# A two-attention, two-expert-layer kernel on one core: second-half result rows gathered by rank under the last pairs

## The chip, the cores and the metric
One core of a Trainium2 chip (trn2). The metric is the device time of one execution in microseconds, median of 3 runs; lower is better.

## What is computed
2048 tokens of 256 features go through attention a, an expert layer, attention b (with latent keys and values) and the expert layer again, each on the layer-normed input and added to it. Cut to the expert layer, on which the change works:

```
logits = x @ gate_w.T
topv, topi = jax.lax.top_k(logits, TOP_K)            # 8 of 64 experts
rw = jax.nn.softmax(topv.astype(jnp.float32), axis=-1)
W = jnp.zeros((N, E)).at[jnp.arange(N)[:, None], topi].set(rw)
gu = jnp.einsum('nh,eih->nei', x, gu_w); gate, up = (gu[..., :I], gu[..., I:])
inter_w = jax.nn.silu(gate) * up * W[:, :, None]
out = jnp.einsum('nei,ehi->nh', inter_w, dp_w)       # I = 64, H = 256
out = out + sigmoid(x @ sh_gate1_w.T) * shared_expert(x)
```

## The kernel before
The engines run five instruction streams that meet only at semaphores. In an expert layer the tokens are worked on in two halves of 8 tiles of 128: first tiles 8 to 15 (half 0), then tiles 0 to 7 (half 1). For each half, the 8192 (token, expert) slots are sorted by expert into blocks of 128 rows, each expert's share rounded up, 128 blocks at most. Two blocks are a pair: pairs 0 to 63 are half 0, pairs 64 to 127 half 1.

- GpSimd (`experts_pool`, L951 on) gathers the sorted token rows by indirect DMA, 64 of 128 rows a half, into a ring of 5 tiles (L1004). TensorE turns each (`turn`, L1368), and ScalarE stores it in `tokensT` (`store`, L1163). Half 1's tiles take the places of half 0's, so their store waits for the pair that read them.
- Per pair: the weights of two experts are copied from `weights` into `fetched` (ring of 3) by ScalarE (`fetch`, L1153) and, for the second block from pair `OTHER_FROM` = 32 on, by DVE (`other`, L1848). TensorE's `gate_up` (L1393), ScalarE's `silu` (L1170), DVE's `gate` (L1858, two operations), TensorE's `down` (L1410), ScalarE's `out` (L1176) into one of two `outs` buffers, and a store of 256 KB from SyncE to `expert_rows` in HBM (L811).
- The sum over a token's 8 experts: for tile t and rank k (the ranks are a token's rows from the last to the first, rank 0 the largest row number) GpSimd gathers 128 rows of `expert_rows` into the same ring (L1009), and DVE adds them to `x`, times the weight (`combine`, L1872). 64 such gathers and adds per half, tile by tile. A gather waits for its ring slot to be added. Half 0's begin when its stores have landed, after the token gathers; half 1's wait for the last store of all.
- Three `rstd` steps for the next norm (`inverse_std`, L947 and L949) stand between half 1's gathers, eight normalisations (L1903) after its 17th add.

The order on TensorE, ScalarE and DVE is not written by hand. `expert_plan` walks its streams of steps, always takes the step that could start first by its table `COST` and its `needs`, and returns the three orders; GpSimd's order is fixed in `experts_pool`. The DVE steps `weights` (L1798 to L1805: routing weights, 16 pieces a half) are among them. Attention b follows: SyncE loads its weights behind the last `down` (L850), and GpSimd splits them after its last `rstd` step.

## Time and profile before
| | us |
|---|---|
| median of 3 runs | 2164.07 (2158.47 to 2185.86) |
| profiled execution, its own time | 2170.09 |
| its span | 2166.8 |
| TensorE / DVE / ScalarE / GpSimd busy | 1704.3 / 1501.8 / 1108.7 / 706.8 |
| mean granted TensorE clock | 0.848 of full |

PE is TensorE, PEld its weight loads, ACT ScalarE, POOL GpSimd, SP SyncE; a q behind a name is the engine's own queue. Spans and starts are in us from the first instruction. A busy share says little of what a stage waits for; that is in the chain, the waits and the timeline of the stage. The counts of instructions are per kernel, so for both layers. "remote" and "issue" are idle times with no releaser that the trace names.

### The profile page before, as it was taken

How to read it: one execution, taken by the hardware profiler on the slowest of the kernel's cores; microseconds unless marked ns; L12 is line 12 of the kernel's file. 1: busy time of each engine (PE TensorE's matmuls, PEld its weight loads, DVE VectorE, ACT ScalarE, POOL GpSimd, SP SyncE). 2: the span in 40 equal slices, each digit the busy share in tenths (PEclk: the TensorE clock that was granted, in tenths of full speed). 3: DMA queues.
4: the chain of work that ended last, by engine and by line, in shares of the span. 5: the costliest groups of instructions: out<-in, count | busy, mean ns of one | idle time of the engine just before them, and what ended most of it. 6: DMA issues, size and time to landing. Idle time of an engine off the chain costs nothing.

```text
span 2166.8 us, 36690 instructions
## 1 busy us (share of the span) xinstructions
PE 1704.3 (79%) x12464; PEld 1097.7 (51%) x12464; DVE 1501.8 (69%) x3241; ACT 1108.7 (51%) x1975; POOL 706.8 (33%) x778
## 2 busy tenths in 40 slices
PE   5799999999767787980197999999997677788920
PEld 4545454445545666770174454544446456677720
DVE  6588888884676744984465788788844767447843
ACT  2145858566355655760041557475662456565710
POOL 5000101001266364547730001010011664554556
PEclk9778989899888999995595789798897789999965
DMA  4640223000444555664244404040004345456643
GB/s 152 139 63 2 38 25 50 12 2 2 175 151 144 161 169 160 209 197 127 68 135 86 56 2 56 6 53 8 2 2 175 121 131 165 152 165 191 207 144 114
DMA packets 123276, 217.59 MB, mean 100 GB/s; under 512 B 16380, under 2 KB 92044, under 8 KB 118812
## 3 DMA queue, kind: packets, MB, share of 16 engines
q1 hardware_dynamic: 98520, 148.10, 25.3%
q0 software_dynamic: 24576, 67.14, 11.1%
q8 instruction: 106, 1.74, 0.4%
q14 instruction: 74, 0.61, 0.1%
HBM read 124.20 MB, written 90.46 MB: 99 GB/s over the span
## 4 chain that ended last, share of the span: by engine, by line
PE 54%; DVE 15%; issue 7%; POOL 7%; DMA 7%; another core or an unknown queue 4%; ACT 4%; SPq 1%; DVEq 1%; ACTq 0%; POOLq 0%
PE late_banks L1575 13%; PE late_banks L1533 11%; PE exp_banks L1561 7%; PE late_banks L1393 6%; PE exp_banks L1410 5%; POOL ring_t L1009 5%; DVE chunk_max_t L1974 3%; DMA expert_rows<-outs_t 3%; PE late_banks L1426 3%; DVE inter_t L1858 2%; PE late_banks L1368 2%; PE late_banks L1539 2%; PE exp_banks L1426 2%; DVE hot_t L1688 2%
## 5 line engine op out<-in xcount | busy, mean ns | idle before, releaser
L1225 ACT ACTIVATE probs_t<-exp_banks 128x1024 f32<-128x1024 f32 (+3 forms) x640 | 538.8, 896 | 342.3 <-PE exp_banks L1561 340.7
L1974 DVE TENSOR_REDUCE chunk_max_t<-late_banks 128x1 f32<-128x512 f32 (+1 forms) x960 | 602.8, 683 | 106.3 <-PE late_banks L1533 86.3
L1084 POOL TENSOR_SCALAR_AFFINE_SELECT probs_t<-probs_t 128x512 f32<-128x512 f32 x128 | 81.2, 635 | 866.6 <-ACT probs_t L1225 866.6
L1393 PE MATMUL late_banks<-tokensT_t,fetched_t 128*128 x2048 | 310.1, 298 | 23.4 <-ACT fetched_t L1153 14.1
L1575 PE MATMUL late_banks<-probs_t,values_t 128*32 128x512 f32 (+3 forms) x2560 | 320.4, 576 | 9.9 <-POOL probs_t L1084 9.5
L1004 POOL DMA_INDIRECT ring_t<-token_rows,index_t x256 | 258.4, 1009 | 201.4 <-PE late_banks L1368 122.8
L1009 POOL DMA_INDIRECT ring_t<-expert_rows,rows_of_t x256 | 243.5, 951 | 196.7 <-DVE x_sb_t L1872 107.7
L1393 PEld LDWEIGHTS late_banks<-tokensT_t,fetched_t 128*128 128x128 f32 x2048 | 267.6, 204 | 52.3 <-issue 39.0
L1858 DVE TENSOR_TENSOR inter_t<-late_banks,silu_t 64x256 f32<-64x256 f32 x512 | 217.3, 424 | 109.3 <-ACT silu_t L1170 60.8
L1533 PE MATMUL late_banks<-contextT_t,Qp_t 50*128 50x512 f32 (+7 forms) x640 | 245.5, 526 | 23.2 <-DVE part_lo_t L1915 10.8
L1410 PE MATMUL exp_banks<-fetched_t,inter_t 64*128 64x128 f32 x2048 | 195.1, 312 | 69.2 <-DVE inter_t L1858 51.9
L1533 PE MATMUL late_banks<-Kp_t,Qp_t 50*128 50x512 f32 (+7 forms) x640 | 221.9, 468 | 2.3 <-DVE chunk_max_t L1974 0.9
L1176 ACT ACTIVATE outs_t<-exp_banks 128x512 f32<-128x512 f32 x256 | 152.0, 594 | 128.6 <-PE exp_banks L1410 59.0
L1410 PEld LDWEIGHTS exp_banks<-fetched_t,inter_t 64*128 64x128 f32 x2048 | 144.0, 199 | 111.4 <-DVE inter_t L1858 63.0
L1872 DVE SCALAR_TENSOR_TENSOR x_sb_t<-ring_t,row_top_t,x_sb_t 128x256 f32<-128x256 f32 x256 | 122.6, 479 | 111.9 <-DMA ring_t<-expert_rows,rows_of_t 106.2
L1533 PEld LDWEIGHTS late_banks<-contextT_t,Qp_t 50*128 50x128 f32 (+1 forms) x640 | 117.2, 226 | 142.0 <-DVE chunk_max_t L1974 94.2
L1533 PEld LDWEIGHTS late_banks<-Kp_t,Qp_t 50*128 50x128 f32 (+1 forms) x640 | 104.5, 203 | 130.9 <-DVE chunk_max_t L1974 98.9
L1153 ACT ACTIVATE fetched_t<-weights_t 128x384 f32 x320 | 158.5, 517 | 15.9 <-issue 13.5
L1561 PE MATMUL exp_banks<-Qp_t,contextT_t 52*128 52x512 f32 (+7 forms) x640 | 149.2, 438 | 16.2 <-DMA Qp_t<-neg_lo_t 12.3
L1848 DVE COPY fetched_t<-weights_t 128x384 f32 x192 | 84.7, 441 | 107.4 <-remote 55.7
L1561 PE MATMUL exp_banks<-Qp_t,Kp_t 52*128 52x512 f32 (+7 forms) x640 | 148.4, 430 | 7.2 <-ACT probs_t L1225 4.9
L1170 ACT ACTIVATE silu_t<-late_banks 64x256 f32<-64x256 f32 x256 | 95.0, 372 | 109.2 <-PE late_banks L1393 63.1
(222 smaller groups left out, 2008.1 us busy)
## 6 DMA issues: line engine op xcount, KB each, us to landing
expert_rows<-outs_t SPq DMA_DIRECT2D x256, 256.0 KB
weights_t<-in_experts SPq DMA_DIRECT2D x8, 1728.0 KB, 14.0
Qp_t<-q_parts SPq DMA_DIRECT2D x36, 256.0 KB
weights_t<-in_experts SPq DMA_DIRECT2D x4, 2112.0 KB, 9.6
Kp_t<-k_parts SPq DMA_DIRECT2D x24, 256.0 KB
q_parts<-part_hi_t SPq DMA_DIRECT2D x16, 256.0 KB, 2.6
q_parts<-part_lo_t SPq DMA_DIRECT2D x16, 256.0 KB, 3.2
k_parts<-part_hi_t SPq DMA_DIRECT2D x16, 256.0 KB, 3.0
```

The source lines that it names most:

```text
L1004: pool.indirect_dma_start(ring[:, slot, :], None, token_rows[f][:, :], bass.IndirectOffsetOnAxis(ap=index[h][:, n:n + 1], axis=0))\
L1009: pool.indirect_dma_start(ring[:, slot, :], None, expert_rows[f][h][:, :], bass.IndirectOffsetOnAxis(ap=rows_of[:, t, k:k + 1], axis=0))\
L1153: act.activation(fetched[:, n % NFETCH, blk, :], weights[:, bass.ds(fetches[n][blk], EW)], ACT.Copy)\
L1176: act.activation(outs[:, out % NOUT, :, :].rearrange("p b (s c) -> p s b c", s=2), down_banks(n).rearrange("p s (b c) -> p s b c", b=2), A ...
L1225: act.activation(probs[:, e % NP, 2 * p:2 * p + 2, off:QB], exp_banks[sq % 2][:, :, off:QB], ACT.Exp, scale=D ** -0.5).then_inc(exp_done, 1)
L1393: last = pe.matmul(bank[:, blk * P:(blk + 1) * P], fetched[:, n % NFETCH, blk, k * P:(k + 1) * P], tokensT[:, bass.ds(starts_of[n][blk] + ...
L1410: last = pe.matmul(down_bank(n, side)[:, blk * P:(blk + 1) * P], inter[rows, n % 2, blk * P:(blk + 1) * P], fetched[rows, n % NFETCH, blk, ...
L1533: last = pe.matmul(bank[:, begin:end], Qp[s][rows, p, t * P:(t + 1) * P], Kp[s][rows, p, c * QB:c * QB + end - begin], start=True, stop=c < b)
L1561: last = pe.matmul(exp_banks[sq % 2][:, hh, off:QB], Kp[s][rows, p, j * P:(j + 1) * P], Qp[s][rows, p, b * QB + off:(b + 1) * QB], start=T ...
L1575: last = pe.matmul(pv_banks[n % NPV][32 * h:32 * h + 32, off:QB], values[:, j, GH * g + h, :], probs[:, e % NP, h, off:QB], start=(j == 0) ...
L1858: dve.tensor_tensor(inter[side * EI:(side + 1) * EI, n % 2, :], up, silu[0:EI, n % 2, :], ALU.mult)\
L1974: op = dve.tensor_reduce(chunk_max[:, slot, p, r, c], bank[:, 0:n].rearrange("q (p k) -> q p k", p=len(parts)), AX.X, ALU.max)
```

## The change
1. `late_order`: half 1's 64 result gathers go by rank, not by tile: ranks 7 to 3, eight tiles each (40), then ranks 2 to 0, one block of four tiles after the other (24). They are issued behind half 0's gathers, in GpSimd's order. Each waits for pair 96 + i/2 to have read its tokens, since 63 of them land in `tokensT`, whose tiles are free by then, and the last in the ring. Two groups of two are open at most.
2. A rank of the first five waits only for the stores up to the largest row that it gathers. These marks are made on the chip: `turn_rows`, `last_rows`, `mark_row` and `marks` (two small TensorE products, six DVE operations), with GpSimd reading them into registers. Ranks 2 to 0 wait for all stores.
3. Half 1's adds leave the planner: DVE does them behind the last pair, after the eight normalisations. Half 0's 64 adds stay in the plan.
4. In half 1, ScalarE copies both weight blocks of every other two pairs (`both_copied`); DVE keeps the rest.
5. The planner's costs are others (landing 2.4 for 2.2, store 3.2 for 2.6, fetch 1.15 for 1.0, and so on), and a store of half 1's tiles is no longer planned 2.5 us behind its pair. Weight pieces 16 to 31 wait for `turn_rows`.
6. `expert_rows` of half 1 is one buffer for both layers, `last_rows_out`; attention a's ScalarE stream fills it once with finite numbers (16 DMAs of 1 MB). Attention b's weights are loaded at add 26 of half 1.

The diff, cut to its core:

```diff
@@ -63,7 +63,10 @@
-GATHERS = 4 * NG
+GATHERS = 3 * NG
+LATE_STEP, LATE_GROUP, LOADED_FROM = 3, 2, 26
+LATE_OPEN = 2
+TURN_ROWS, MARK_ROW = 33, 37
@@ -72,6 +75,7 @@
+BOTH_OF = 4
@@ -280,12 +284,25 @@
+def both_copied(n):
...
+    return n < OTHER_FROM or n >= NPAIR and n % BOTH_OF < 2
...
+def late_order():
...
+    order = [(t, k) for k in range(TOPK - 1, LATE_STEP - 1, -1) for t in HALVES[1]]
+    for b in range(HT // TPB):
+        order += [(t, k) for k in range(LATE_STEP - 1, -1, -1) for t in HALVES[1][b * TPB:(b + 1) * TPB]]
+    return order
...
-    LAND, STORED, LOADED, SIGNAL, BEHIND = 2.2, 2.6, 6.0, 0.15, 2.5
-    COST = {"gather": 1.25, "turn": 0.45, "gate_up": 1.2, "down": 0.75, "index": 0.65, "table": 0.6, "fetch": 1.0,
-            "store": 0.4, "silu": 0.4, "out": 0.61, "gate": 0.86, "other": 0.58, "columns": 3.4, "low": 1.25, "high": 1.2, "index_out": 0.3,
-            "places": 2.2, "table_out": 0.5, "rows": 2.2, "shares": 4.0, "weights": 1.4, "combine": 0.5}
+    LAND, STORED, LOADED, SIGNAL = 2.4, 3.2, 6.0, 0.15
+    COST = {"gather": 1.27, "turn": 0.45, "gate_up": 1.2, "down": 0.75, "index": 0.65, "table": 0.6, "fetch": 1.15,
+            "store": 0.4, "silu": 0.4, "out": 0.61, "gate": 0.88, "other": 0.6, "columns": 3.4, "low": 1.29, "high": 1.42, "index_out": 0.3,
+            "places": 2.2, "table_out": 0.5, "turn_rows": 0.4, "mark_row": 0.4, "last_rows": 1.0, "marks": 1.2, "rows": 2.2, "shares": 4.0, "weights": 1.4, "combine": 0.5}
@@ -303,8 +322,8 @@
                ("dve", [("gate", n) for n in pairs]),
-               ("dve", [("other", n) for n in pairs if n >= OTHER_FROM]),
-               ("dve", [("combine", n) for n in range(2 * NG)]),
+               ("dve", [("other", n) for n in pairs if not both_copied(n)]),
+               ("dve", [("combine", n) for n in range(NG)]),
@@ -363,7 +392,7 @@
             if n >= NG:
-                yield "gate_up", n // 2, BEHIND
+                yield "gate_up", n // 2, 0.0
@@ -565,7 +604,8 @@
         token_rows = [nc.dram_tensor(f"token_rows{f}", [S, E], F32).ap() for f in range(2)]
-        expert_rows = [[nc.dram_tensor(f"expert_rows{f}{h}", [NBLK * P, E], F32).ap() for h in range(2)] for f in range(2)]
+        last_rows_out = nc.dram_tensor("last_rows_out", [NBLK * P, E], F32).ap()
+        expert_rows = [[nc.dram_tensor(f"expert_rows{f}", [NBLK * P, E], F32).ap(), last_rows_out] for f in range(2)]
@@ -745,7 +791,18 @@
+        def late_tile(i):
...
+            at = i % KC * (SLOTS + P) + i // KC * E
+            return tokensT[:, at:at + E] if i < NG - 1 else ring[:, 0, :]
@@ -846,7 +907,7 @@
                 if layer == 1:
-                    sp.wait_ge(down_done, layer * PAIRS)
+                    sp.wait_ge(combined, layer * 2 * NG - NG + LOADED_FROM)
@@ -986,15 +1047,12 @@
                 slot, h, n = m % NRING, m // NG % 2, m % NG
-                place = pool_norms.get(m)
-                if place is not None:
-                    inverse_std(pool, norm_of["f", f] + 1, place)
...
-                    pool.wait_ge(rows_ready, 2 * f + h + 1)
-                    for i in range(NOUT):
-                        pool.wait_ge(outs_out[i], 16 * ((f * 2 * NPAIR + (h + 1) * NPAIR - i + NOUT - 1) // NOUT))
+                    pool.wait_ge(rows_ready, 2 * f + 2)
+                    for out in outs_out:
+                        pool.wait_ge(out, 16 * ((f * PAIRS + NPAIR) // NOUT))
@@ -1009,7 +1067,34 @@
                         .then_inc(ring_in[slot], 16)
-            for place in range(3, NB):
+            pool.wait_ge(rows_ready, 2 * f + 2)
+            pool.wait_ge(marked, f + 1)
...
+            written = [*low_marks, *high_marks]
+            for i, (t, k) in enumerate(LATE):
+                if i in LATE_NORMS:
+                    inverse_std(pool, norm_of["f", f] + 1, LATE_NORMS[i])
+                pool.wait_ge(gate_up_done, f * PAIRS + NPAIR + NPAIR // 2 + i // 2 + 1)
+                if i % LATE_GROUP == 0 and i >= LATE_OPEN * LATE_GROUP:
+                    pool.wait_ge(late_in[i // LATE_GROUP - LATE_OPEN], 16 * LATE_GROUP * (f + 1))
+                if i == NG - 1:
+                    pool.wait_ge(combined, f * 2 * NG + NG)
+                if i < (TOPK - LATE_STEP) * HT:
+                    if i % HT == 0:
+                        for out in outs_out:
+                            pool.wait_ge(out, written[k])
+                elif i == (TOPK - LATE_STEP) * HT:
+                    for out in outs_out:
+                        pool.wait_ge(out, 16 * ((f + 1) * PAIRS // NOUT))
+                pool.indirect_dma_start(late_tile(i), None, expert_rows[f][1][:, :],
+                                        bass.IndirectOffsetOnAxis(ap=rows_of[:, t, k:k + 1], axis=0))\
+                    .then_inc(late_in[i // LATE_GROUP], 16)
+            for place in range(2, NB):
@@ -1038,6 +1123,8 @@
                     inverse_std(pool, 0, b)
+                if layer == 1:
+                    pool.wait_ge(combined, layer * 2 * NG)
@@ -1149,7 +1236,7 @@
                         act.wait_ge(down_done, f * PAIRS + n - NFETCH + 1)
-                    for blk in range(2 if n < OTHER_FROM else 1):
+                    for blk in range(2 if both_copied(n) else 1):
@@ -1232,6 +1319,10 @@
                         act.activation(sums[:, n % 2, :], pv_banks[n % NPV][:, :], ACT.Copy).then_inc(sums_out, 1)
+                        if layer == 0:
+                            rows = slice(n * NBLK * P // len(BLOCKS), (n + 1) * NBLK * P // len(BLOCKS))
+                            act.dma_start(last_rows_out[rows, :].rearrange("(p r) e -> p (r e)", p=P),
+                                          values[:, 0:TPB, :, :].rearrange("p t h d -> p (t h d)")).then_inc(rows_set, 16)
@@ -1356,6 +1447,17 @@
                     table_row(1, BANK[3])
+                elif kind == "turn_rows":
+                    pe.wait_ge(out_ready, f * PAIRS + TURN_ROWS + 1)
+                    pe.wait_ge(row_done[1], HT * (f + 1))
+                    tiles = slice(HALVES[1].start, HALVES[1].stop)
+                    pe.transpose(BANK[3][0:NEXP, PW:PW + P], row_top[:, tiles, :].rearrange("p t k -> p (t k)"), ident[:, :])\
+                        .then_inc(rows_turned, 1)
+                elif kind == "mark_row":
+                    pe.wait_ge(out_ready, f * PAIRS + MARK_ROW + 1)
+                    pe.wait_ge(mark_step, 5 * f + 2)
+                    pe.matmul(BANK[3][:, PW + P:PW + P + NEXP], last_rows, ident[EI:P, EI:P], start=True, stop=True)\
+                        .then_inc(mark_product, 1)
@@ -1790,6 +1897,8 @@
                 h, first = i // PIECES, i % PIECES * EQ
+                if i == PIECES:
+                    dve.wait_ge(rows_turned, f + 1)
@@ -1812,7 +1921,28 @@
-            others = {}
+            def last_rows_of():
...
+                dve.wait_ge(rows_turned, f + 1)
+                dve.tensor_reduce(last_row, BANK[3][0:NEXP, PW:PW + P], AX.X, ALU.max).then_inc(mark_step, 1)
+                dve.wait_ge(mark_step, 5 * f + 1)
+                dve.tensor_scalar(last_rows, ident[EI:P, :], 0.0, last_row, ALU.mult, ALU.add).then_inc(mark_step, 1)
...
+            def marks_of():
...
+                dve.wait_ge(mark_product, f + 1)
+                dve.tensor_reduce(row_steps[0], BANK[3][0:1, PW + P:PW + P + NEXP].rearrange("o (t k) -> o k t", t=HT), AX.X, ALU.max)\
+                    .then_inc(mark_step, 1)
+                dve.wait_ge(mark_step, 5 * f + 3)
...
@@ -1860,11 +1996,11 @@
                 elif kind == "combine":
-                    h, t, k = n // NG, HALVES[n // NG][n % NG // TOPK], n % TOPK
+                    t, k = HALVES[0][n // TOPK], n % TOPK
...
-                    if n % NG == 0:
-                        dve.wait_ge(weights_done, 2 * f + h + 1)
+                    if n == 0:
+                        dve.wait_ge(weights_done, 2 * f + 1)
@@ -1874,10 +2010,23 @@
                         statistics(phase, t // TPB)
-                    if n == NG + 16:
-                        dve.wait_ge(down_done, (f + 1) * PAIRS)
-                        for b in MIDDLE[0:2]:
-                            normalise(phase, b)
+            dve.wait_ge(down_done, (f + 1) * PAIRS)
+            for b in MIDDLE[0:2]:
+                normalise(phase, b)
+            dve.wait_ge(weights_done, 2 * f + 2)
+            last = {}
+            for i, (t, k) in enumerate(LATE):
+                n = f * 2 * NG + NG + i
+                if i % LATE_GROUP == 0:
+                    dve.wait_ge(late_in[i // LATE_GROUP], 16 * LATE_GROUP * (f + 1))
+                if t in last:
+                    dve.wait_ge(combined, last[t])
+                dve.scalar_tensor_tensor(out=x[:, t, :], in0=late_tile(i), scalar=weight8[:, t, k:k + 1],
+                                         in1=x[:, t, :], op0=ALU.mult, op1=ALU.add).then_inc(combined, 1)
+                last[t] = n + 1
+                if k == 0 and t % TPB == TPB - 1:
+                    dve.wait_ge(combined, n + 1)
+                    statistics(phase, t // TPB)
```

How the order moves. GpSimd, layer 0, from the second token gather of half 1 on; `token_rows` are the tokens, `expert_rows` and `last_rows_out` the pairs' results. Before:

```order
L1004 DMA ring_t<-token_rows,index_t 128x256 [waits tile_turned] x63
L1009 DMA ring_t<-expert_rows,rows_of_t 128x256 [waits outs_out1,tile_turned,outs_out0,rows_ready]
L1009 DMA ring_t<-expert_rows,rows_of_t 128x256 [waits tile_turned] x4
L1009 DMA ring_t<-expert_rows,rows_of_t 128x256 [waits combined] x59
L1009 DMA ring_t<-expert_rows,rows_of_t 128x256 [waits outs_out1,combined,outs_out0,rows_ready]
L1009 DMA ring_t<-expert_rows,rows_of_t 128x256 [waits combined] x7
L947 TENSOR_SCALAR var_eps_t<-mean_var_t 128x4 [waits aggr_done]
L949 TENSOR_TENSOR rstd_t<-var_eps_t,minus_half_t 128x4 [waits eps_done]
L1009 DMA ring_t<-expert_rows,rows_of_t 128x256 [waits combined] x4
L947 TENSOR_SCALAR var_eps_t<-mean_var_t 128x4 [waits aggr_done]
L949 TENSOR_TENSOR rstd_t<-var_eps_t,minus_half_t 128x4 [waits eps_done]
```

And now:

```order
L1062 DMA ring_t<-token_rows,index_t 128x256 [waits tile_turned] x63
L1067 DMA ring_t<-expert_rows,rows_of_t 128x256 [waits outs_out1,tile_turned,outs_out0,rows_ready]
L1067 DMA ring_t<-expert_rows,rows_of_t 128x256 [waits tile_turned] x4
L1067 DMA ring_t<-expert_rows,rows_of_t 128x256 [waits combined] x59
L1072 TENSOR_LOAD silu_t [waits marked,rows_ready]
L1075 TENSOR_LOAD silu_t
L1094 DMA tokensT_t<-last_rows_out,rows_of_t 128x256 [waits outs_out1,outs_out0,gate_up_done]
L1094 DMA tokensT_t<-last_rows_out,rows_of_t 128x256 [waits gate_up_done] x3
L1008 TENSOR_SCALAR var_eps_t<-mean_var_t 128x4 [waits aggr_done]
L1010 TENSOR_TENSOR rstd_t<-var_eps_t,minus_half_t 128x4 [waits eps_done]
L1094 DMA tokensT_t<-last_rows_out,rows_of_t 128x256 [waits late_in0,gate_up_done]
L1094 DMA tokensT_t<-last_rows_out,rows_of_t 128x256 [waits gate_up_done]
```

The 64 gathers of half 0 (waiting for `combined`) stay where they were; the 64 behind them wait for `gate_up_done` instead of `combined`.

DVE around pairs 102 to 104 of layer 0, where L1872 (now L2008) is an add, L1858 (now L1994) a pair's gate and L1848 (now L1984) a weight copy. Before:

```order
L1872 SCALAR_TENSOR_TENSOR x_sb_t<-ring_t,row_top_t,x_sb_t 128x256
L1858 TENSOR_TENSOR inter_t<-late_banks,silu_t 64x256 x2
L1843 TENSOR_LOAD silu_t
L1848 ISA
L1848 COPY fetched_t<-weights_t 128x384
L1872 SCALAR_TENSOR_TENSOR x_sb_t<-ring_t,row_top_t,x_sb_t 128x256
L1858 TENSOR_TENSOR inter_t<-late_banks,silu_t 64x256 x2
```

And now:

```order
L1994 TENSOR_TENSOR inter_t<-late_banks,silu_t 64x256 x2
L1984 ISA
L1984 COPY fetched_t<-weights_t 128x384
L2008 SCALAR_TENSOR_TENSOR x_sb_t<-ring_t,row_top_t,x_sb_t 128x256 x2
L1994 TENSOR_TENSOR inter_t<-late_banks,silu_t 64x256 x2
L2008 SCALAR_TENSOR_TENSOR x_sb_t<-ring_t,row_top_t,x_sb_t 128x256 x2
L1994 TENSOR_TENSOR inter_t<-late_banks,silu_t 64x256 x2
L2008 SCALAR_TENSOR_TENSOR x_sb_t<-ring_t,row_top_t,x_sb_t 128x256 x2
L2041 BN_STATS stats_t<-x_sb_t 128x6 x4
L2044 BN_AGGR mean_var_t<-stats_t 128x2 x4
```

Before, one add a pair, and copies in each; now one or two adds at each gate, copies in two pairs of four, and half 0's adds are over here (the statistics are its last block's).

DVE behind the last pair of layer 0: L1903 (now L2052) is the normalisation. Before:

```order
L1858 TENSOR_TENSOR inter_t<-late_banks,silu_t 64x256 x2
L1872 SCALAR_TENSOR_TENSOR x_sb_t<-ring_t,row_top_t,x_sb_t 128x256 x17
L1903 TENSOR_SCALAR xn_t<-x_sb_t,mean_var_t,rstd_t 128x256 x8
L1872 SCALAR_TENSOR_TENSOR x_sb_t<-ring_t,row_top_t,x_sb_t 128x256 x15
L1892 BN_STATS stats_t<-x_sb_t 128x6 x4
L1895 BN_AGGR mean_var_t<-stats_t 128x2 x4
L1872 SCALAR_TENSOR_TENSOR x_sb_t<-ring_t,row_top_t,x_sb_t 128x256 x32
L1892 BN_STATS stats_t<-x_sb_t 128x6 x4
L1895 BN_AGGR mean_var_t<-stats_t 128x2 x4
L1903 TENSOR_SCALAR xn_t<-x_sb_t,mean_var_t,rstd_t 128x256 x8
```

And now:

```order
L1994 TENSOR_TENSOR inter_t<-late_banks,silu_t 64x256 x4
L2052 TENSOR_SCALAR xn_t<-x_sb_t,mean_var_t,rstd_t 128x256 x8
L2024 SCALAR_TENSOR_TENSOR x_sb_t<-tokensT_t,row_top_t,x_sb_t 128x256 x52
L2041 BN_STATS stats_t<-x_sb_t 128x6 x4
L2044 BN_AGGR mean_var_t<-stats_t 128x2 x4
L2024 SCALAR_TENSOR_TENSOR x_sb_t<-tokensT_t,row_top_t,x_sb_t 128x256 x11
L2024 SCALAR_TENSOR_TENSOR x_sb_t<-ring_t,row_top_t,x_sb_t 128x256
L2041 BN_STATS stats_t<-x_sb_t 128x6 x4
L2044 BN_AGGR mean_var_t<-stats_t 128x2 x4
L2052 TENSOR_SCALAR xn_t<-x_sb_t,mean_var_t,rstd_t 128x256 x8
```

Before, 17 adds, the normalisations, 47 adds; now the normalisations and then all 64.

## Rows read from the trace of the kernel before
**Rows 1.** The page's part 4, whole span: share of the chain by engine
```profile
PE 54%; DVE 15%; issue 7%; POOL 7%; DMA 7%; another core or an unknown queue 4%; ACT 4%; SPq 1%; DVEq 1%; ACTq 0%; POOLq 0%
```

**Rows 2.** Busy us by stage: PE, PEld, DVE, ACT, POOL (xcount); PEclk, DMA share, GB/s
```profile
749.50:846.60 97.10, 76.33 (x636) 64.06 (x635) 42.98 (x111) 58.04 (x159) 54.79 (x57) 0.95 0.53 165
846.60:928.70 82.10, 73.27 (x644) 61.94 (x645) 68.69 (x169) 54.01 (x121) 42.20 (x45) 0.96 0.64 199
...
974.10:1064.30 90.20, 3.55 (x16) 3.27 (x16) 35.24 (x81) 2.96 (x5) 65.14 (x70) 0.52 0.38 114
...
2077.10:2162.60 85.50, 0.00 (x0) 0.00 (x0) 31.01 (x64) 0.60 (x1) 60.49 (x64) 0.52 0.41 122
```

**Rows 3.** The chain in order of time behind layer 0's last pair: start, us, what
```profile
974.07 0.61 ACT outs_t L1176
...
974.70 2.14 DMA expert_rows<-outs_t
...
1061.05 0.95 POOL ring_t L1009
```

**Rows 4.** Timeline, ends of both layers: start, us, engine, line, op, tiles, idle before
```profile
977.66 0.94 POOL L1009 DMA_INDIRECT ring_t<-expert_rows,rows_of_t  x1 [12.79 <-DMA expert_rows<-outs_t]
...
1063.75 0.48 DVE L1872 SCALAR_TENSOR_TENSOR x_sb_t<-ring_t,row_top_t,x_sb_t 128x256 f32<-128x256 f32 x1 [0.81 <-DMA ring_t<-expert_rows,rows_of_t]
...
2158.15 0.95 POOL L1009 DMA_INDIRECT ring_t<-expert_rows,rows_of_t  x1 [0.30 <-issue]
...
2159.40 0.94 POOL L1009 DMA_INDIRECT ring_t<-expert_rows,rows_of_t  x1 [0.30 <-issue]
...
2162.13 0.48 DVE L1872 SCALAR_TENSOR_TENSOR x_sb_t<-ring_t,row_top_t,x_sb_t 128x256 f32<-128x256 f32 x1 [0.74 <-DMA ring_t<-expert_rows,rows_of_t]
```

**Rows 5.** Timeline where layer 0's first result-row gathers run
```profile
848.43 0.94 POOL L1009 DMA_INDIRECT ring_t<-expert_rows,rows_of_t  x1 [9.29 <-DMA expert_rows<-outs_t]
...
851.68 0.48 DVE L1872 SCALAR_TENSOR_TENSOR x_sb_t<-ring_t,row_top_t,x_sb_t 128x256 f32<-128x256 f32 x1
```

**Rows 6.** Result-row gathers (L1009) under the pairs, layer 0, then layer 1
```profile
L1009 POOL DMA_INDIRECT ring_t<-expert_rows,rows_of_t x63: 940/944/1142, 849.7 to 963.9; - x63
...
  DVE x_sb_t L1872: 50.7, 49
...
L1009 POOL DMA_INDIRECT ring_t<-expert_rows,rows_of_t x64: 940/940/1141, 1947.9 to 2067.8; - x64
```

**Rows 7.** `outs` copies (L1176, one a pair) in three stretches of layer 0
```profile
749.50:846.60 97.10, 18.86 (x32) 0.95 0.53 165
846.60:928.70 82.10, 23.84 (x41) 0.96 0.64 199
928.70:974.70 46.00, 14.29 (x24) 1.00 0.62 193
```

**Rows 8.** GpSimd's timeline, token gathers under the first half's last pairs
```profile
778.65 0.99 POOL L1004 DMA_INDIRECT ring_t<-token_rows,index_t  x1 [1.41 <-PE late_banks L1368]
...
784.80 0.99 POOL L1004 DMA_INDIRECT ring_t<-token_rows,index_t  x1 [1.40 <-PE late_banks L1368]
```

**Rows 9.** The page's part 5: weight copies by ScalarE and by DVE
```profile
L1153 ACT ACTIVATE fetched_t<-weights_t 128x384 f32 x320 | 158.5, 517 | 15.9 <-issue 13.5
...
L1848 DVE COPY fetched_t<-weights_t 128x384 f32 x192 | 84.7, 441 | 107.4 <-remote 55.7
```

**Rows 10.** DVE's weight copies while gathers run, layer 0
```profile
L1848 DVE COPY fetched_t<-weights_t x58: 359/516/570, 849.2 to 964.5; 128x384 f32 x58
```

**Rows 11.** ScalarE's waits in layer 1's second half: for whom, us in total, times, longest
```profile
ACT outs_t L1176 <- DMA expert_rows<-outs_t: 16.1, 22, 2.2
...
ACT silu_t L1170 <- remote: 3.4, 1, 3.4
```

**Rows 12.** Attention a: busy us by engine, and TensorE's longest wait for a DMA
```profile
150.00:500.00 350.00, 344.96 (x2560) 166.10 (x2562) 301.47 (x565) 230.30 (x274) 29.17 (x46) 0.91 0.15 20
...
PE exp_banks L1561 <- DMA Qp_t<-neg_lo_t: 4.5, 3, 3.0
```

90 lines of the change are left out of this document (75 added, 15 removed).

## Prediction
> **What bounds the kernel now.** I read the chain of waits first. Over the whole span TensorE has 54% of it, but GpSimd has 7% and DMA 7% [rows 1], and cut to stages they sit in two places: behind the last pair of each expert layer. There the table by stage shows TensorE at 3.6 us of 90.2 in layer 0 and at nothing of 85.5 in layer 1, while GpSimd is busy 60 to 65 us [rows 2]. In order of time the chain there is: ScalarE's last `outs` copy at 974.07, its store landed 2.14 us after 974.70, then one result-row gather after the other up to 1061.05 [rows 3]. The ends of both stages read alike: gathers start 1.25 us apart, DVE adds each one as it lands, and the last add starts 2.73 us after the last gather (2159.40 to 2162.13) [rows 4]. So 64 gathers of the second half, about 80 us, stand alone twice; that is the stretch at stake. Adds take 0.48 us and wait for the landing each time, so DVE isn't the limit there.
>
> Next, what the gathers of the first half do, since they come first in GpSimd's order. They start at 848.43, the first add at 851.68 [rows 5], and the 63 from 849.7 to 963.9 are 1.84 us apart though one takes 0.94; 50.7 us of their idle time is ended by DVE's adds, whose places in DVE's order stand one per pair [rows 6]. The pairs: the `outs` copies count 32 in 749.5 to 846.6, 41 in the next 82.1 us and 24 in the last 46 [rows 7]: 3.03, 2.0 and 1.92 us a pair. None of the three engines is full there (DVE 68.7 of 82.1, PE 73.3, ACT 54.0) [rows 2]. So pair 64 (the second half's first) is at 846.6, pair 104 at about 928.7, the last at 974.07.
>
> **The change part by part.**
> 1. *Half 0's gathers and adds, packed.* The plan now puts adds 0 to 63 by the gate step of pair 103 instead of 127. The order of GpSimd doesn't move. Ring of five: a slot is back after landing and add, 851.68 + 0.48 - 848.43 = 3.7 us [rows 5], against 5 x 1.25 = 6.25 us for five gathers, so 2.5 us are left for an add to wait its turn on DVE. I take 1.30 us a gather (bounds: 1.25, the idle pitch, and 1.84, today's): 64 x 1.30 = 83.2 us. DVE in pairs 64 to 103: 27 more adds by pair 103 (64 against 37) at 0.48 = 13.0 us [rows 4], and 20 fewer weight copies at 0.441 = 8.8 [rows 9]: 68.7 + 4.2 = 72.9 of 82. It fits, without much room. ScalarE takes those copies over: 20 x 0.517 = 10.3, 64.3 of 82 [rows 2, 9].
> 2. *40 gathers of ranks 7 to 3 under the pairs.* They begin when half 0's end: 848.43 + 83.2 = 931.6, about pair 105. Their data conditions: counted on these inputs by the reference's routing, the marks let rank 7 go when pairs up to 87 are stored, rank 6 at 99, ranks 5 to 3 at 101 to 105, each before its gathers' turn. The slot condition (pair 96 + i/2 has read its tokens) is met too. Four open: gather 2i waits for 2i - 3, issued three pitches before, 3.75 us against about 3.2 for a landing [rows 5]; again 1.30: 52 us. The two `rstd` steps between them cost what they cost now, (1061.05 - 977.66 - 63 x 1.25)/3 = 1.5 us each [rows 3, 4]. Done at 931.6 + 52 + 3.1 = 986.7. That is after the last store's landing today (976.84), so the remaining 24 don't wait.
> 3. *24 gathers of ranks 2 to 0*: the last starts 23 x 1.25 = 28.8 us later, 1015.5; its add at + 2.73 = 1018.2. Today 1063.75 [rows 4]: 45.5 us less in layer 0. Layer 1, from 1947.9 [rows 6] and with no `rstd` steps: 1947.9 + 83.2 + 52 + 28.8 + 2.7 = 2114.6 against 2162.13: 47.5 less. Together 93.
> 4. *What is late next.* All 64 adds of half 1 now stand behind the last pair on DVE, and eight normalisations before them. If they start at 974 and cost 5 us and 64 x 0.48 to 0.59, they end at 1010 to 1017: just below GpSimd's 1018. And if the pairs end late by d, ranks 2 to 0 go at 977.7 + d and end at 1009 + d: a delay of the pairs is free up to 9 us. Behind the last add everything stays as it is: `rstd`, normalisation, turn; the load of attention b's weights moves from the last pair to add 26 of half 1, some 15 us later, and still has more than 20 us before GpSimd splits them.
> 5. *Stalls in the packed stretch.* Pairs, adds and gathers hold each other with 2.5 us of play. ScalarE stops once for 3.4 us there already, with no releaser that the trace names [rows 11]. Bounds 0 and 10 us a layer; I take 4, so +8.
> 6. *Pairs 0 to 63, new order.* 16 weight pieces (three DVE operations each) move from pairs 21 to 37 to pairs 35 to 51, where a pair takes 3.03 us and DVE is busy 43 of 97 [rows 2]. The turns of half 1's tiles stand one pair earlier on TensorE. In that stretch GpSimd waits 1.4 us for a turn at 778.65 and again at 784.80 [rows 8]: 6.15 us for four gathers and two pairs, where four gathers alone would take 5.0. If the new order takes that wait out, a pair costs 2.5 to 2.6: 32 x 0.45 = 14 us a layer; if the new turns catch a landing later, the same is lost in part. Bounds -14 and +6 a layer; I take -2, near today's rows: -4.
> 7. *Preparing.* 16 DMAs on ScalarE's queue in attention a write 16.8 MB of finite data to the new buffer. DMA is busy 15% in that stage [rows 12]; ScalarE is busy 230 of 350 us there. +1. The marks: two small products and six small DVE operations, under 5 us in all, in the stretch of part 6: 0.
>
> Sum: 93 - 8 + 4 - 1 = 88. The profiled execution took 2170.1 (span 2166.8), 6 us above the median of 2164.1. 2170.1 - 88 = 2082; on the median's basis 2076.
>
> One rule speaks against laying software gathers under DVE work. The 63 gathers that ran under the pairs have a median of 944 ns and a maximum of 1142 [rows 6], the lone ones 940 to 950 [rows 4]; the copies beside them have a median of 516 ns and a minimum of 359 [rows 10]. So here the copy pays 0.16 us, and the gather nothing. The Trainium skill's page "SBUF — State Buffer", section "SBUF: two separate sides", says that an fp32 copy between SBUF tiles on DVE locks GpSimd out of the shared port pair so that it can't write descriptors, and "A bandwidth-pool intuition that's wrong" gives about 3.1 us for a gather so covered against 0.62 alone; by that the covered gathers would be slower by 2.5 us at each such copy. By that rule, the trace does not agree, as an estimate for these sizes.
>
> **The rivals.**
> A. *The packed gathers slow the pairs.* For it: today 16.1 us of ScalarE's waits in pairs 64 to 127 of layer 1 are for a store of `outs` to land [rows 11], DMA is at 0.64 [rows 2], and gathers come in 1.30 instead of 1.84 us; ScalarE gets half the second copies and is then close to TensorE's 1.7 us a pair. Against: the share stays below three quarters. If these waits double, pairs end 16 us later a layer, 7 to 16 of which count: about 2108.
> B. *The first half gains.* Part 6 at its good bound, 14 a layer instead of 2, and no stalls: 2076 - 24 - 6 = about 2046. For it: the regular 1.4 us wait [rows 8]. Against: the other waits of that pattern are not explained by the order.
> C. *The change doesn't pack the gathers.* If 1.84 us is landing and queueing and not the adds' places, the adds' new places drag the pairs along: 64 x 1.84 = 118 instead of 83, 35 us a layer, 93 - 70 = 23: 2138 with part 7. Against it: 1.25 within the first gathers [rows 5] and a landing of 3.2 us. The lock rule above would end here.
> D. *Slower than before.* Attention a's 16.8 MB. At the rate of today's stores (256 KB in 2.14 us [rows 3]) it is 64 x 2.14 = 137 us of transfers. Each block's row maxima go by small DMAs into `Qp` before its scores start; TensorE waits only 4.5 us for them today [rows 12]. If each write held those small transfers for its whole length, 137 us would come on the path: 2076 + 137 = 2213. It decides against the change from two thirds of that on (88 of 137). Against: different queue, DMA at 15%, and a store in flight doesn't stop today's gathers, which land in 3 us beside it.
>
> **How the numbers follow.** Forecast 0.52, A 0.20, B 0.20, C 0.05, D 0.03. Predicted 2076. The range goes from B's 2046 rounded down to 2044, up past A to 2114, half of what lies between A and C; outside are C, D and the rims. A difference of 2% (43 us) is what this kernel's measurement tells from none, so faster means below 2121: forecast, A and B, 0.92. Within 2%: C, 0.05. Slower: D, 0.03.
>
> **What would show it.** In the changed profile: the last add less than 50 us behind the last `outs` copy (90 now); gathers of half 0 1.25 to 1.4 us apart and over by pair 105; then 40 gathers into `tokensT` before the last store; the granted clock low for a shorter stretch. A is right if pairs 64 to 127 take over 135 us (127.5 now), B if pairs 32 to 63 take under 88 (97). The forecast is wrong if GpSimd waits long for `outs_out` or for a landing under the pairs, if DVE's adds outlast GpSimd by over 5 us, or if attention a grows by more than 5 us.

## The result, and the profile after

The changed kernel took 2241.2 us (median of four, 2238.4 to 2247.0), the kernel before 2171.7 on the same chip (four runs): ratio 1.033, 95% interval 1.029 to 1.037. Slower, where the forecast was 2076 and faster. The profiled execution has a span of 2236.6 us, 69.8 more than before.

The table by stage of the changed kernel answers to [rows 2] (busy us of PE, PEld, DVE, ACT, POOL, then TensorE's granted clock, the share of DMA and GB/s). The stretches are: layer 0's pairs 32 to 63, 64 to 103, 104 to 127 and what lies behind the last pair; then the last three for layer 1.

```profile
760.80:863.80 103.00, 82.64 (x635) 68.55 (x633) 58.00 (x151) 58.88 (x160) 54.13 (x56) 0.88 0.50 155
863.80:985.80 122.00, 85.71 (x640) 72.32 (x640) 74.10 (x181) 61.79 (x140) 70.81 (x72) 0.83 0.53 161
985.80:1061.50 75.70, 50.39 (x360) 42.46 (x360) 24.72 (x63) 33.67 (x77) 34.30 (x37) 0.75 0.46 143
1061.50:1110.90 49.40, 3.68 (x16) 3.28 (x16) 28.61 (x75) 2.94 (x5) 37.14 (x26) 0.50 0.33 103
1983.80:2124.40 140.60, 93.59 (x656) 78.99 (x656) 70.82 (x165) 61.53 (x141) 80.52 (x82) 0.75 0.49 151
2124.40:2185.00 60.60, 45.95 (x344) 38.66 (x344) 22.71 (x55) 33.65 (x76) 21.51 (x23) 0.79 0.47 148
2185.00:2233.30 48.30, 0.00 (x0) 0.00 (x0) 26.49 (x64) 0.60 (x1) 35.08 (x24) 0.53 0.35 109
```

The stretch that was at stake did shrink, from 90 and 85 us [rows 2] to 49 and 48. But pairs 64 to 103 take 122 and 141 us instead of 82 and 85, and pairs 104 to 127 76 and 61 instead of 45. Of the engines only GpSimd got much more work there (71 us of gathers in layer 0's pairs 64 to 103 instead of 42 [rows 2]). DVE is busy 74 of 122 us, and TensorE's 640 products take 86 us where they took 73 [rows 2]; the granted clock fell from 0.96 to 0.83.

Half 0's gathers answer to [rows 6]: planned at 1.30 us, they came at (975.7 - 865.2)/63 = 1.75.

```profile
L1067 POOL DMA_INDIRECT ring_t<-expert_rows,rows_of_t x64: 943/949/1208, 865.2 to 975.7; - x64
its engine sat idle before it (us, times) until:
  DVE x_sb_t L2008: 34.9, 22
```

What the pairs do there is seen in the timeline, here under layer 0's late gathers (start, us, engine, line, operation, tiles, idle before it and what ended that):

```profile
1001.82 0.95 POOL L1094 DMA_INDIRECT tokensT_t<-last_rows_out,rows_of_t  x1 [0.30 <-issue]
1002.38 1.78 PEld L1495 LDWEIGHTS late_banks<-tokensT_t,fetched_t 128*128 128x128 f32 x8 [0.22 <-issue]
1002.38 2.07 PE L1495 MATMUL late_banks<-tokensT_t,fetched_t 128*128 x8
...
1006.73 1.23 PE L1516 MATMUL exp_banks<-fetched_t,inter_t 64*128 64x128 f32 x8 [2.28 <-issue]
...
1011.04 0.60 ACT L1263 ACTIVATE outs_t<-exp_banks 128x512 f32<-128x512 f32 x1 [5.28 <-remote]
1011.14 0.36 DVE L1984 COPY fetched_t<-weights_t 128x384 f32 x1 [4.46 <-remote]
```

TensorE's eight `down` products stand drawn from 1006.73 to 1007.96, but the ScalarE copy that needs only them starts at 1011.04, and DVE's weight copy, which waits for the same products, at 1011.14. The profile only models where a product ends; both that wait for it got its signal 3 us later. I call a *stop* any time over 1.5 us in which neither ScalarE nor DVE works. Before had 1 and 2 stops in pairs 64 to 127 of the two layers, 9 us in all; after has 12 and 16, 80 us in all. A stop is often followed by a low clock: one at 871.3 to 873.8, half clock from 873.3 to 880.1.

Behind the last pair a second thing is to be seen that no row of before shows:

```profile
1062.09 15.92 DVE L2024 SCALAR_TENSOR_TENSOR x_sb_t<-tokensT_t,row_top_t,x_sb_t 128x256 f32<-128x256 f32 x40
...
1064.89 13.94 POOL L1094 DMA_INDIRECT tokensT_t<-last_rows_out,rows_of_t  x1 [29.43 <-DMA last_rows_out<-outs_t]
...
1079.13 0.94 POOL L1094 DMA_INDIRECT tokensT_t<-last_rows_out,rows_of_t  x1 [0.30 <-issue]
```

The first gather of ranks 2 to 0 takes 13.94 us where others take about 0.95, and it ends at 1078.83, 0.8 us behind DVE's unbroken chain of 40 adds (1078.01).

### The profile page after: what moved, and what is told of

Read it like the earlier page. It is cut to its first block, busy times and chain, and to the rows that moved or that the text cites. A ratio compares the mean times of both kernels' runs of the same rounds, so it can differ in the third digit from the quotient of the medians.

```text
span 2236.6 us, 36726 instructions
## 1 busy us (share of the span) xinstructions
PE 1773.1 (79%) x12470; PEld 1148.5 (51%) x12470; DVE 1473.1 (66%) x3189; ACT 1133.0 (51%) x2039; POOL 737.9 (33%) x778
## 4 chain that ended last, share of the span: by engine, by line
PE 56%; DVE 14%; issue 9%; another core or an unknown queue 7%; ACT 5%; DMA 5%; POOL 2%; SPq 1%; DVEq 0%; ACTq 0%; POOLq 0%
PE late_banks L1682 12%; PE late_banks L1640 10%; PE late_banks L1495 8%; PE exp_banks L1668 7%; PE exp_banks L1516 6%; PE late_banks L1533 3%; DVE chunk_max_t L2123 3%; PE late_banks L1470 3%; DVE inter_t L1994 2%; PE late_banks L1646 2%; PE exp_banks L1533 2%; DVE hot_t L1795 2%; DMA Qp_t<-neg_lo_t 1%; ACT probs_t L1312 1%
## 5 line engine op out<-in xcount | busy, mean ns | idle before, releaser
L2123 DVE TENSOR_REDUCE chunk_max_t<-late_banks 128x1 f32<-128x512 f32 (+1 forms) x960 | 602.9, 683 | 116.6 <-PE late_banks L1640 93.8
L1495 PE MATMUL late_banks<-tokensT_t,fetched_t 128*128 x2048 | 345.6, 321 | 33.6 <-issue 29.6
L1994 DVE TENSOR_TENSOR inter_t<-late_banks,silu_t 64x256 f32<-64x256 f32 x512 | 217.8, 425 | 215.3 <-ACT silu_t L1257 145.9
L1495 PEld LDWEIGHTS late_banks<-tokensT_t,fetched_t 128*128 128x128 f32 x2048 | 298.6, 224 | 69.2 <-issue 59.1
L1516 PE MATMUL exp_banks<-fetched_t,inter_t 64*128 64x128 f32 x2048 | 217.8, 339 | 118.6 <-DVE inter_t L1994 105.0
L1640 PE MATMUL late_banks<-contextT_t,Qp_t 50*128 50x512 f32 (+7 forms) x640 | 251.2, 537 | 22.1 <-DVE part_lo_t L2064 10.9
L1516 PEld LDWEIGHTS exp_banks<-fetched_t,inter_t 64*128 64x128 f32 x2048 | 162.3, 221 | 163.8 <-DVE inter_t L1994 119.2
L1240 ACT ACTIVATE fetched_t<-weights_t 128x384 f32 x384 | 184.4, 516 | 10.8 <-issue 10.1
L1094 POOL DMA_INDIRECT tokensT_t<-last_rows_out,rows_of_t x126 | 145.9, 1158 | 109.5 <-DMA last_rows_out<-outs_t 59.8
L1067 POOL DMA_INDIRECT ring_t<-expert_rows,rows_of_t x128 | 127.6, 997 | 122.6 <-DVE x_sb_t L2008 73.3
L1470 PE MATMUL late_banks<-ident_t,ring_t 128*128 128x128 f32 x512 | 103.0, 316 | 69.8 <-ACT tokensT_t L1250 47.6
```

Source lines behind the costliest of these rows:

```text
L1240: act.activation(fetched[:, n % NFETCH, blk, :], weights[:, bass.ds(fetches[n][blk], EW)], ACT.Copy)\
L1470: last = pe.transpose(bank[:, k * P:(k + 1) * P], ring[:, slot, k * P:(k + 1) * P], ident[:, :])
L1495: last = pe.matmul(bank[:, blk * P:(blk + 1) * P], fetched[:, n % NFETCH, blk, k * P:(k + 1) * P], tokensT[:, bass.ds(starts_of[n][blk] + ...
L1516: last = pe.matmul(down_bank(n, side)[:, blk * P:(blk + 1) * P], inter[rows, n % 2, blk * P:(blk + 1) * P], fetched[rows, n % NFETCH, blk, ...
L1640: last = pe.matmul(bank[:, begin:end], Qp[s][rows, p, t * P:(t + 1) * P], Kp[s][rows, p, c * QB:c * QB + end - begin], start=True, stop=c < b)
L1994: dve.tensor_tensor(inter[side * EI:(side + 1) * EI, n % 2, :], up, silu[0:EI, n % 2, :], ALU.mult)\
```

## The experiments

The experiments ran on five chips, and these came in two kinds: the kernel before took 2097, 2101 and 2086 us on three of them, 2173 and 2178 on two (medians). The recorded result (2172) is of the second kind. I call them 2100 chips and 2170 chips; what makes them differ isn't known. Each kernel is compared with before on its own chip. In the tables, times are us of layer 0 / layer 1; the tail is from the last pair's `outs` copy to the last add.

| on 2100 chips | pairs 64-103 | 104-127 | tail | ratio to before, 95% |
|---|---|---|---|---|
| before (e7_before) | 76.3 / 76.2 | 44.1 / 42.4 | 90.1 / 85.1 | |
| e6_after: as changed | 93.7 / 93.1 | 48.0 / 46.0 | 51.8 / 48.9 | 0.982, 0.978-0.987 |
| e1_hold | 94.2 / 92.0 | 45.7 / 44.1 | 92.8 / 87.3 | 1.019, 1.012-1.026 |
| e4_hold_nofill | 93.9 / 94.4 | 44.5 / 43.2 | 92.2 / 87.5 | 1.019, 1.013-1.026 |
| e3_copies | 76.8 / 76.1 | 42.7 / 40.7 | 87.5 / 83.8 | 1.001, 0.997-1.005 |
| e5_spaced | 78.0 / 80.3 | 43.1 / 44.6 | 81.9 / 77.0 | 0.997, 0.994-1.000 |
| e8_looser | 83.6 / 87.0 | 50.0 / 44.4 | 60.0 / 56.3 | 0.989, 0.982-0.996 |
| e9_open1 | 93.8 / 92.6 | 46.0 / 44.1 | 117.5 / 115.3 | 1.042, 1.035-1.048 |
| e18_ring | 90.3 / 91.2 | 46.7 / 47.4 | 98.6 / 91.1 | 1.034, 1.027-1.041 |
| e19_under | 94.1 / 93.0 | 46.2 / 49.0 | 42.6 / 38.2 | 0.973, 0.967-0.980 |

| on 2170 chips | pairs 64-103 | 104-127 | tail | ratio to before, 95% |
|---|---|---|---|---|
| before | 82.1 / 85.2 | 45.4 / 45.9 | 89.7 / 85.0 | |
| after (the result) | 122.1 / 140.6 | 75.6 / 60.7 | 49.0 / 47.8 | 1.033, 1.029-1.037 |
| e13_again: as changed | 124.8 / 130.2 | 76.2 / 70.8 | 49.2 / 47.7 | 1.043, 1.033-1.053 |
| e17_hold | 123.2 / 120.0 | 42.3 / 42.4 | 93.0 / 87.2 | 1.036, 1.029-1.043 |
| e16_spaced | 86.9 / 88.6 | 49.2 / 93.8 | 75.7 / 47.8 | 1.008, 1.004-1.012 |
| e10_under | 126.3 / 125.4 | 73.9 / 76.1 | 38.4 / 36.0 | 1.030, 1.024-1.036 |
| e15_under | 119.2 / 123.1 | 75.2 / 75.4 | 36.5 / 35.9 | 1.018, 1.013-1.023 |
| e14_loose_under | 108.7 / 112.7 | 83.9 / 87.5 | 42.5 / 39.8 | 1.022, 1.014-1.029 |
| e12_three | 109.6 / 110.8 | 87.1 / 90.7 | 42.6 / 39.9 | 1.056, 1.048-1.064 |
| e11_fillearly | 125.5 / 131.0 | 76.8 / 70.6 | 49.0 / 47.8 | 1.064, 1.058-1.071 |

**Hold the late gathers back.**

```diff
-                pool.wait_ge(gate_up_done, f * PAIRS + NPAIR + NPAIR // 2 + i // 2 + 1)
+                pool.wait_ge(gate_up_done, (f + 1) * PAIRS)
...
-                if i < (TOPK - LATE_STEP) * HT:
-                    if i % HT == 0:
-                        for out in outs_out:
-                            pool.wait_ge(out, written[k])
-                elif i == (TOPK - LATE_STEP) * HT:
+                if i == 0:
```

> The changed kernel, but the 64 late gathers wait for the last pair and all its stores; orders on PE, ACT and DVE are word for word those of the changed kernel. Theory L (the late gathers slow the pairs they run under): pairs 104 to 127 come back from 76 and 61 us to the 45 of before, pairs 64 to 104 stay at 122 and 141 us since they run before the first late gather; the 64 gathers then stand alone (tail 90 and 86 us instead of 49 and 48), so 2241 - 46 + 79 = about 2274. Theory P (the planned orders and the packed adds slow all pairs from 64 on, the late gathers do nothing): pairs 104 to 127 stay at 76 and 61, and the time is 2241 + 79 = 2320.

e4_hold_nofill is the same with the fill taken out:

```diff
-            sp.wait_ge(rows_set, 16 * len(BLOCKS))
...
-                            act.dma_start(last_rows_out[rows, :].rearrange("(p r) e -> p (r e)", p=P),
-                                          values[:, 0:TPB, :, :].rearrange("p t h d -> p (t h d)")).then_inc(rows_set, 16)
```

> As the run before it, and without the 16 DMAs that fill last_rows_out during attention a (all rows are written before the first gather here, so nothing needs them). Theory F (each fill holds up the small row-maxima DMAs behind it): pair 0 of layer 0 starts 11 us earlier (632.5 instead of 643.8), the rest is the same: 11 us below e1_hold. Rival (the 11 us come from somewhere else, a different instruction layout say): no difference to e1_hold.

Neither theory's numbers came, since this first chip was another one: 2133 us against 2097. Pairs 64 to 103 took 94 and 92 us without a single stop. Without the fill (2137) nothing was gained; theory F fell in this comparison. Theories L and P are told apart on a 2170 chip further down (e17_hold).

**The split of the copies, and the packing.** First with before's rule for the copies, then with the new rule and the adds spaced.

```diff
 def both_copied(n):
-    return n < OTHER_FROM or n >= NPAIR and n % BOTH_OF < 2
+    return n < OTHER_FROM
```

```diff
         elif kind == "combine":
             yield "gather", 2 * NG + n, LAND
+            yield "gate", NPAIR + n, 0.0
```

> The changed kernel with before's rule for the weight copies: from pair 32 on the second copy of every pair is DVE's, no longer ScalarE's in pairs 64, 65, 68, 69 and so on. With it the planner places half 0's adds one per pair up to pair 127, as before; the late gathers then come behind the last pair. Theory P: pairs 64 to 104 take 82 to 85 us again, pairs 104 to 127 45 us; late gathers start at the last pair, tail about 90: time about before + 11 for the fill, 2175 to 2190. If the slow pairs come from the new costs, marks or the token row buffers and not from copies or packing: pairs 64 to 104 stay over 110 us and the time is above 2240.

> The changed kernel with its new split of weight copies kept, but half 0's adds planned one per pair (add n not before the gate step of pair 64 + n), so the gathers are not packed and the late ones come behind the last pair. If the packing (two adds between gate steps, each waiting for a landing) slows the pairs: pairs 64 to 104 take 82 to 88 us, time 2175 to 2195. If the new split of copies (ScalarE with both copies of every second couple of pairs) does it: pairs 64 to 104 stay at 110 us or more, time 2250 or more.

Both give 76 to 80 us on the chip on which e1_hold took 94 and 92. So packing alone costs some 15 us a layer there, without stops, and it is not the split of the copies, the costs or the marks.

**The changed kernel and the one before, on a 2100 chip.**

> The changed kernel as it is, on the chip of this call. On the chip of the four runs before, pairs 64 to 127 stand still nowhere (no stretch over 1.5 us without work on ACT and DVE), where the recorded trace of the changed kernel has 28 such stops. Theory S (the stops belong to that first chip and the change only met more of them): no stops here, pairs 64 to 104 take 94 us as with held gathers, tail about 50: e1_hold less 2 x 40, about 0.98 of before. Theory L (the late gathers and what comes with them make the stops, anywhere): stops again, pairs 104 to 127 over 60 us, ratio 1.02 or more.

> The kernel before, for its trace on this chip. Half 0's gathers at 1.8 us, pairs 64 to 104 about 77 us, pairs 32 to 64 about 97 us if the new order gained 14 us there, 83 if the chip alone makes the difference between 97 and 83; tail about 88.

Theory S held: one stop, of 1.7 us, ratio 0.982. The same program is 1.8% faster than before here, on the one 2100 chip on which it ran, and slower on both 2170 chips. Pairs 32 to 63 are 82.5 and 80.2 us in before here, 84.5 and 81.3 in the changed kernel: 97 to 82 was the chip, and the new order of part 6 gained nothing. Layer 0 of the changed kernel, then of before, in four stretches each (pairs 32 to 63, 64 to 103, 104 to 127, tail):

```profile
754.00:838.20 84.20, 74.87 (x632) 61.02 (x632) 58.93 (x150) 58.60 (x159) 53.95 (x56) 0.98 0.63 190
838.20:931.90 93.70, 74.53 (x642) 62.61 (x643) 72.24 (x181) 61.97 (x141) 69.04 (x72) 0.96 0.69 209
931.90:979.70 47.80, 41.38 (x360) 34.48 (x359) 24.88 (x62) 33.29 (x76) 31.15 (x33) 0.96 0.70 213
979.70:1031.90 52.20, 3.35 (x16) 3.12 (x16) 28.68 (x75) 2.93 (x5) 41.66 (x30) 0.53 0.36 110
```

```profile
746.50:829.00 82.50, 73.45 (x637) 60.13 (x637) 41.80 (x110) 60.20 (x159) 54.24 (x57) 1.00 0.64 194
829.00:905.20 76.20, 70.43 (x641) 59.73 (x642) 68.05 (x168) 53.52 (x120) 42.10 (x44) 1.00 0.69 210
905.20:949.30 44.10, 39.26 (x360) 33.18 (x360) 39.43 (x99) 29.87 (x66) 19.12 (x20) 1.00 0.67 207
949.30:1039.90 90.60, 3.67 (x16) 3.27 (x16) 35.11 (x80) 2.99 (x5) 65.44 (x70) 0.53 0.38 114
```

Here the packed gathers do run at (922.8 - 839.5)/63 = 1.32 us. In the view of waits GpSimd now hardly waits for adds (of the changed kernel, pairs 64 to 103: who waited, for whom, us, times, longest):

```profile
ACT outs_t L1263 <- PE exp_banks L1516: 22.9, 28, 2.9
PEld exp_banks L1516 <- DVE inter_t L1994: 22.2, 21, 2.7
...
DVE x_sb_t L2008 <- DMA ring_t<-expert_rows,rows_of_t: 11.1, 12, 1.9
...
POOL ring_t L1067 <- DVE x_sb_t L2008: 7.5, 17, 1.2
```

Before, on the same chip, it is the other way round:

```profile
POOL ring_t L1009 <- DVE x_sb_t L1872: 28.1, 31, 2.3
...
PEld exp_banks L1410 <- DVE inter_t L1858: 4.7, 5, 2.2
```

So gathers used to wait for DVE, and now DVE waits for landings 12 times, 11.1 us, with the gate steps queued behind it and TensorE behind those: 22 us instead of 5. How far DVE's own load has a part isn't separated: from pair 67's gate step to pair 103's it is busy 65 of 84 us, against 63 of 70 in before and 56 of 71 in e5_spaced (layer 0).

**Looser packing; fewer gathers open.**

```diff
+            yield "gate", NPAIR + n * 3 // 4, 0.0
```

```diff
-LATE_OPEN = 2
+LATE_OPEN = 1
```

> The changed kernel with half 0's adds planned three for four pairs (done by pair 111 instead of 103). If the packing costs by how close the adds stand, pairs 64 to 104 lose about half of what they lose in the changed kernel (86 instead of 94 us where there are no stops), and the late gathers start 10 us later, at pair 112: tail about 60. So within 5 us of the changed kernel in a chip without stops, and clearly faster (over 1%) where stops come with packing.

> The changed kernel with at most two late gathers open instead of four: each pair of gathers waits for the landing of the pair before. If open gathers crowd the DMA queues or buffers and so make the stops: fewer stops, faster than the changed kernel by over 1%. If not: late gathers come every (3.2 + 1.25) / 2 = 2.2 us instead of 1.3, so the tail grows by up to 24 x 0.9 = 22 us a layer plus what no longer fits under the pairs: 1.5 to 2.5% slower than the changed kernel.

With three adds for four pairs the pairs win back 10 and 6 us and the tail gives back 8 and 7: a trade, no gain (2078 us against 2065, where I had expected them within 5). Two gathers open instead of four cost 128 us in all, 6% where I had at most 2.5%: the late gathers come 2.5 to 2.8 us apart, under the pairs too, where only 18 to 20 instead of 36 fit. As the changed kernel has next to no stops on this chip, e9_open1 doesn't say whether fewer open gathers would take stops away. Looser packing doesn't: on 2170 chips (e12_three, e14_loose_under) pairs 64 to 103 keep 5 to 7 stops a layer.

**The long gather.** 30 late adds go from behind the last pair to behind the gate steps, two at a time. In these kernels attention b's weight load also waits for the last `down` again, as it did before.

```diff
+            late_at = {105 + 3 * g // 2: g for g in range(15)}
...
                 elif kind == "gate":
...
+                    if n in late_at:
+                        if late_at[n] == 0:
+                            dve.wait_ge(weights_done, 2 * f + 2)
+                        late_add(2 * late_at[n])
+                        late_add(2 * late_at[n] + 1)
```

> The changed kernel, with 30 of the 64 late adds moved from behind the last pair to behind the gate steps of pairs 105 to 126, two at a time. In the changed kernel one gather takes 12 to 15 us (0.95 otherwise) while DVE runs some 38 adds without a gap behind the last pair. Theory K (the unbroken chain of adds keeps GpSimd from writing its descriptors): the long gather is gone or under 4 us, the tail falls from 49 to 52 us to 38 to 41, the kernel is 15 to 25 us faster than the changed one on the same chip. Rival (the long gather is the profile's drawing, or it waits for the landing of the stores): it stays, no gain; or the adds, waiting for landings in DVE's order, make pairs 104 to 127 longer by as much as the tail falls.

> The kernel of e10_under again (30 late adds behind gate steps). On a chip near 2100: theory K has the one long gather gone and 20 to 25 us off the changed kernel's 2065: 2040 to 2045, 0.972 of before, faster than both. On a chip near 2170: 2234 again.

> The kernel of e10_under a third time. If the chip is one near 2100: 2040 to 2045, about 0.972 of before, faster than before and by 20 us faster than the changed kernel on e6_after's chip (0.982). If it is one near 2170: 1.02 to 1.03.

Theory K's numbers came each time: the long gather is under 4 us, and the tail is 36 to 43 us. In e10_under the chain behind the last pair is 10 adds long, 4.04 us, and the gather lasts to its end and 0.8 us more:

```profile
1075.49 4.04 DVE L1955 SCALAR_TENSOR_TENSOR x_sb_t<-tokensT_t,row_top_t,x_sb_t 128x256 f32<-128x256 f32 x10
...
1076.49 3.86 POOL L1095 DMA_INDIRECT tokensT_t<-last_rows_out,rows_of_t  x1 [26.69 <-DMA last_rows_out<-outs_t]
```

With 20 fewer adds (e14_loose_under) it takes 7.97 us in layer 0 and 5.34 in layer 1, in the changed kernel 11.9 to 14.8. In all of them it ends 0.8 us behind the chain, so the chain holds it. But not every gather in a chain is held. In layer 1 of e8_looser three pass through a chain of 28 adds before one is:

```profile
2011.94 11.17 DVE L2025 SCALAR_TENSOR_TENSOR x_sb_t<-tokensT_t,row_top_t,x_sb_t 128x256 f32<-128x256 f32 x28 [0.82 <-PE exp_banks L1517]
...
2016.25 0.95 POOL L1095 DMA_INDIRECT tokensT_t<-last_rows_out,rows_of_t  x1 [1.36 <-issue]
2017.50 6.43 POOL L1095 DMA_INDIRECT tokensT_t<-last_rows_out,rows_of_t  x1 [0.30 <-issue]
```

And in layer 0 of e1_hold four gathers begin in a run of four normalisations and 14 adds and take 0.95 to 1.24 us. What picks the one that is held isn't shown.

The tail falls by 11 to 12 us on the 2170 chip and by 9 and 11 on the 2100 chip. There (two chips of the kind) the kernel (e19_under) takes 2039 us against 2086 of before and is the best of all: 0.973. On 2170 chips it stays slower than before.

**The fill.** The 16 writes become eight copies of the input x from DRAM, issued at the start; e12_three adds this to looser packing and 20 moved adds, e14_loose_under is the same with the old fill.

```diff
+                if layer == 0:
+                    for i in range(NBLK * P // S):
+                        act.dma_start(last_rows_out[i * S:(i + 1) * S, :], A["x"]).then_inc(rows_set, 16)
```

> The changed kernel with the new buffer filled by 8 copies of the input x, 2 MB each, from DRAM, early in attention a, instead of 16 writes of values between its score blocks. Theory F (the fills hold up the row-maxima DMAs): attention a ends 5 to 12 us earlier than in the changed kernel, the rest is the same: 0.4% faster. Rival (its length varies by as much from run to run, with or without the fill): under 3 us between the medians.

> Three edits at once, as a candidate that may beat both kernels: half 0's adds planned three for four pairs, 20 late adds behind gate steps from pair 112 on, the early fill. If the three costs (adds denser than gathers come, the chain that holds a gather, the fill) are separate: pairs 64 to 104 84 us, tail 45, attention a 8 us shorter: 15 to 30 us below the changed kernel on the same chip, 0.97 of before. If they are one and the same, no gain over the changed kernel.

> The changed kernel with half 0's adds planned three for four pairs and 20 late adds behind gate steps from pair 112 on; the fill as in the changed kernel. On a chip whose kernel before takes about 2100 us: pairs 64 to 104 take 84 us, tail 45: 2050, 0.975 of before. On a chip whose kernel before takes about 2170 us: 110, 87 and 42 us as in e12_three, without its 48 us at the start: 2240, 1.03.

Worse by 52 us (2308 against e13_again's 2256): DMA moves 210 to 370 GB/s from 30 to 110 us of e11_fillearly (means of 10 us), beside the first projections, and attention a is 48 us behind before it reaches its score blocks (the first product with `Qp` at 125.1 us against 76.7). e12_three comes to 2292 us, no gain over the changed kernel; e14_loose_under to 2220 (2240 expected). What the fill costs where it is, is best told from all traces with it: pair 0 of layer 0 starts at 635 to 660, mean 648 (15 traces), against 632.5, 636.5 and 637.5 in the three without it. Some 12 us by the traces (e11_fillearly and e12_three are left out of the 15), though the one direct comparison of medians doesn't show it: 2133 us with the fill (e1_hold), 2137 without (e4_hold_nofill). Row maxima that wait behind the fill are at most a part: near 155 us TensorE waits 3.7 to 5.5 us for such a transfer in 14 of the 15 traces with the fill, and in one of the three without it, for 3.5 us. Where the rest comes from isn't shown.

**On 2170 chips again: which part makes the stops?**

> The changed kernel unchanged, again, for its ratio and stops on the chip of this call. By theory S (the 28 stops of the first trace belong to the chip on which it ran): 0.98 of before without stops, or, if this chip shows stops in the kernel before as well (before near 2165 instead of 2100), stops in pairs 64 to 127 and a ratio over 1.02.

> The kernel of e5_spaced again (one add of half 0 per pair, late gathers all behind the last pair). On a chip near 2170 it tells what makes the stops: if the packed adds do, pairs 64 to 104 take 82 to 88 us with 0 to 3 stops and the kernel is within 1% of before; if the new split of the weight copies does, they take 120 us or more with 10 stops. On a chip near 2100: 0.997 again.

> The kernel of e1_hold again (packed adds, late gathers behind the last pair). On a chip near 2170: if the late gathers make the stops of 3 to 8 us in pairs 104 to 127, these pairs take 45 to 50 us here instead of 61 to 76, while pairs 64 to 104 stay at 120 to 140. If the stops go on by themselves once the packed adds have started them, or if they come with the orders, pairs 104 to 127 stay over 60. On a chip near 2100: 1.019 again.

The 28 stops came back with the chip: 13 and 16. With spaced adds pairs 64 to 103 take 87 and 89 us and have 1 and 2 stops; packed, they have 7 and 6 and take 123 and 120 even without a late gather. With the late gathers held back, pairs 104 to 127 have no stop and take 42 us at full clock, as theory L had it. e17_hold, layer 0, pairs 64 to 103 and 104 to 127:

```profile
865.30:988.50 123.20, 88.29 (x643) 74.59 (x641) 73.63 (x181) 61.39 (x140) 63.52 (x64) 0.81 0.50 155
988.50:1030.90 42.40, 39.65 (x362) 33.32 (x360) 22.50 (x56) 34.03 (x77) 0.00 (x0) 1.00 0.39 138
```

So packing makes the stops in the first stretch and the late gathers those in the second; each goes when its part is taken out. e16_spaced shows it once more, unplanned: in its layer 1 all 40 late gathers of ranks 7 to 3 still ran under pairs 104 to 127, and these took 94 us, with stops of 15 and 17. In its layer 0 ten late gathers under the last pairs made none.

**Does it matter where the late gathers write?** Forty more gathers under the pairs, into `ring` instead of `tokensT`, which TensorE is reading.

```diff
+                pool.indirect_dma_start(ring[:, i % NRING, :], None, expert_rows[f][1][:, :],
+                                        bass.IndirectOffsetOnAxis(ap=rows_of[:, t, k:k + 1], axis=0))\
+                    .then_inc(again_in[g % 2], 16)
```

> The kernel of e1_hold (all 64 late gathers behind the last pair) with 40 more gathers under pairs 104 to 127, under the same waits as the late gathers of the changed kernel, but into the ring of five buffers instead of into tokensT; nothing reads them. On a chip near 2170: if it matters that the late gathers write tokensT, which TensorE reads for the products of these same pairs, there are no stops over 3 us here and pairs 104 to 127 take 42 to 50 us as in e17_hold. If any gather under these pairs with nothing that paces it stops TensorE: stops of 3 to 8 us and 61 to 76 us, as in the changed kernel. On a chip near 2100: 46 us in both cases. The whole is slower than e1_hold by at most what is left of the 40 gathers behind the last pair, 0 to 15 us a layer.

It came on a 2100 chip, where neither target makes stops of more than 1.7 us (pairs 104 to 127 take 46.7 and 47.4 us). This stays open.

## Why the prediction was wrong

The table follows the path through both layers; sums are us, each worked out from the starts of pairs (their `outs` copies) and the last adds in the traces of the changed kernel and of before on a chip of the kind, and rounded by itself.

| stretch | predicted | 2170 chip | 2100 chip |
|---|---|---|---|
| up to pair 0 | +1 | +11 | +12 |
| pairs 0-63, both layers | -4 | +5 | -3 |
| pairs 64-103 | +8, stalls | +95 | +34 |
| pairs 104-127 | 0 | +45 | +7 |
| tails | -93 | -78 | -75 |
| between layers, and the end | 0 | -9 | -10 |
| sum | -88 | +70 | -34 |

Two steps failed: part 1, on both kinds of chip, and part 5's bound, which on the chip of the result turned a gain into a loss.

*Part 1 failed.* "It fits, without much room" compared busy times, and 83.2 us of gathers with the 82 us of pairs 64 to 103. But the adds start only behind pair 67's gate step and must be over by pair 103's: 36 pairs, at 1.92 to 2.05 us some 70 to 74 us, for 64 gathers that take 80 at 1.25 us. DVE takes its steps in order, so the pairs had to slow to the gathers' pace: on the 2100 chip that stretch took 84.0 and 83.5 us, 64 gathers of 1.32 us, where before took 69.5 and 69.3. That was in [rows 5, 7] and in the order; rival C names this mechanism, but only for gathers at 1.84 us. It is worth 34 us on the 2100 chip, and e5_spaced takes most of it out (28). With the fill and the long gather it leaves a gain of 34 us of the forecast's 88: 2164 - 34 = 2130, above the range's 2114 even without stops.

*Part 5's bound of 10 us a layer for stalls was wrong on the 2170 chips*: 40 and 55 us more there in pairs 64 to 103, of which the drag seen on 2100 chips explains 17 each, then 30 and 15 in pairs 104 to 127. Of these 140 us the stops over 1.5 us are 72 (80 less before's 9) and the drag some 34; the rest, the time at the lower clock included, isn't divided further. The clue was at hand: one 3.4 us wait with no releaser [rows 11], and twelve more stops in pairs 0 to 63 of layer 0. I took them for a constant of the kernel. Rival A (chance 0.20) had the right sign for the pairs and the wrong cause: it isn't stores that land late.

*Parts 2 and 3 were right in mechanism.* The marks let the gathers go, and 36 to 40 of them ran under the pairs, at 1.5 us. The tails are 48 to 52 us, against the 44 and 37.5 of the steps. That they came so close is in part luck: the long gather, 13 us a layer, was not in the sum, but the pairs were so late that on the 2170 chip all 40 gathers were issued before the last copy, where part 2 had the last of them done 10 us behind the last store.

*The rule that I weighed and set aside is what part 4 lacks.* [rows 10] showed single copies beside single gathers, and there the gathers paid nothing. Part 4's own edit put DVE's adds into an unbroken chain, which [rows 4], with an add each 1.25 us, could not show. One gather begun inside that chain was held to its end: 15.9 us of adds, 13.94 of gather. The Trainium skill's page "SBUF — State Buffer", section "SBUF: two separate sides", describes the port pair that DVE and GpSimd share as "an **exclusive lock**, not a bandwidth split", and counts a DVE op with two SBUF inputs among those that take it against a GpSimd op that reads SBUF. By that rule, the trace agrees only in part: that section speaks of one instruction at a time, while a gather was held through 40 adds, others in a chain weren't held, and the lone copies held none. That moving the adds shortens the gather is shown; that the port pair is the reason isn't.

*Between the layers* nothing was forecast; 9 and 10 us less were measured, but that stretch (last add to the next pair 0) varies from 647 to 669 us over all traces, so I read nothing into it.

*Part 6*: nothing was gained in pairs 32 to 63 (B fell); all pairs 0 to 63 came out at +5 and -3 where -4 was forecast. *Part 7*: pair 0 starts 11 to 12 us later instead of 1; the traces put it down to the fill, the medians of e1_hold and e4_hold_nofill don't. D's mechanism isn't shown; its 137 us didn't come.

*What the signs said.* In the result the last add came less than 50 us behind the last copy, as the forecast had it, and half 0's gathers were over by pair 105, but 1.75 and 1.82 us apart instead of 1.25 to 1.4. The granted clock was lower and not higher, 0.825 against 0.848 over the span. The sign of A (over 135 us for pairs 64 to 127, 198 and 201 here) came too, and so did one sign of a wrong forecast: up to pair 0 it took 11 us more, over the 5 allowed.

## What to carry to other kernels

Before packing work into an in-order engine, compare the time that the feeding engine needs with the time of the steps that it must stand between (here 80 us against 36 pairs, some 72 us), not with the length of the stage: an add that waits for its landing makes every step behind it wait. Where GpSimd must issue gathers behind the last pair, look for a long run of DVE adds beside them, and try to break the run up. And time a close change on more than one chip: this one is 1.8% faster on one kind and 3 to 4% slower on the other.

## What the runs showed that I had not expected

- On 2170 chips TensorE's products come late when gathers are issued almost without a pause beside them: the longest stop is 6 us in the result, 8 to 12 in e13_again, e10_under and e14_loose_under, 17 in e16_spaced. In e16_spaced, ten gathers went out 1.25 us apart while one pair's `gate_up` stood finished in the drawing at 2108.91; ScalarE had it at 2121.72. Where adds pace the gathers at 1.9 us, or none run, stops are rare, and 25 of before's 28 stops lie in pairs 0 to 63, where token gathers run. It isn't the whole rule: the ten late gathers in layer 0 of e16_spaced, 1.45 us apart, made no stop. What the gathers hold up in TensorE was not shown. Loading of instructions doesn't end the stop shown here: the only instruction packet in the DMA records from 2104 to 2126 starts at 2122.66, behind it.

```profile
2106.84 2.07 PE L1496 MATMUL late_banks<-tokensT_t,fetched_t 128*128 x8 [6.43 <-issue]
...
2121.37 0.95 POOL L1095 DMA_INDIRECT tokensT_t<-last_rows_out,rows_of_t  x1 [0.30 <-issue]
2121.72 0.38 ACT L1258 ACTIVATE silu_t<-late_banks 64x256 f32<-64x256 f32 x1 [15.12 <-remote]
```

- Stops and the low clock go together there. In the result's layer 1 the clock is at its lower level (0.5, 1.2 GHz) for 6.8 us from 1992.9, 2006.5, 2020.2 and 2033.8; stops began at 1989.7, 2004.5, 2020.5 and 2032.5, three ahead of the fall and one with it. After the first three the next stop came 5 to 7 us after the clock was back, after the fourth 1.6 us. Which brings the other isn't shown.
- DMA's mean share doesn't make it the limit on 2170 chips: it is lower there in pairs 64 to 103 (0.53) than on a 2100 chip (0.69), as is its rate (161 against 209 GB/s).
